# A graph network's node layout: eight consecutive nodes per partition instead of every 128th

## The reference

```python
h = x
for i in range(L):
    hw = jnp.einsum('bnc,cd->bnd', h, weight[i])
    m = jnp.einsum('bjn,bjd->bnd', adj, hw)
    gx = m @ w_ih[i].T + b_ih[i]; gh = h @ w_hh[i].T + b_hh[i]
    xr, xz, xn = split(gx, 3); hr, hz, hn = split(gh, 3)
    r = sigmoid(xr + hr); z = sigmoid(xz + hz)
    n = tanh(xn + r * hn)
    h = (1 - z) * n + z * h
x = layernorm(x + h * mask[:, :, None], axis=-1)   # eps 1e-5
```

## Time and profile before

| | |
|---|---|
| median of 3 runs | 538.66 us (538.38 to 539.0) |
| the profiled execution | 537.98 us |
| its span, first to last instruction | 536.2 us |
| busy: PE / DVE / ACT / POOL | 514.1 / 386.1 / 384.6 / 221.2 us |
| DMA | 85.13 MB, mean 159 GB/s |

### The profile page before, as it was taken

One profiled execution on the slowest core, in us unless ns is written; L12 is line 12 of the kernel. 1 busy time (PEld: TensorE's weight loads), 2 busy tenths in 40 slices (PEclk: granted clock), 3 DMA queues, 4 the chain that ended last, 5 costly groups with the idle time before them and its releaser, 6 DMA issues.

```text
span 536.2 us, 7420 instructions
## 1 busy us (share of the span) xinstructions
PE 514.1 (96%) x2288; PEld 421.5 (79%) x2288; DVE 386.1 (72%) x678; ACT 384.6 (72%) x638; POOL 221.2 (41%) x162
## 2 busy tenths in 40 slices
PE   6999999999999999999999999999999999999970
PEld 4688888888888888888888888888888888888760
DVE  3787666666788886666689886567688887667585
ACT  4668777749776788856886877984986777985444
POOL 2045232344345454432336554232355454344443
PEclk9999999999999999999999999999999999999996
DMA  8941553255732356273662256356472165524212
GB/s 307 382 190 53 213 194 138 91 165 156 238 136 80 122 185 224 82 226 111 198 246 82 65 205 215 117 169 183 137 274 80 60 216 174 185 74 146 90 60 82
DMA packets 78896, 85.13 MB, mean 159 GB/s; under 512 B 3768, under 2 KB 61712, under 8 KB 78864
## 3 DMA queue, kind: packets, MB, share of 16 engines
q1 hardware_dynamic: 78864, 84.73, 47.5%
HBM read 64.27 MB, written 20.45 MB: 158 GB/s over the span
## 4 chain that ended last, share of the span: by engine, by line
PE 92%; DMA 1%; POOL 1%; DVE 1%; issue 1%; SPq 1%; ACT 1%; POOLq 0%; DVEq 0%; ACTq 0%
PE p_S L508 40%; PE p_r L518 6%; PE p_r L522 5%; PE p_r L519 5%; PE p_z L518 5%; PE p_z L522 5%; PE p_z L519 5%; PE p_hn L518 3%; PE p_hn L522 3%; PE p_hn L519 3%; PE p_xn L522 3%; PE p_xn L519 3%; PE p_xn L518 3%; DMA adj_in<-in_adj_dram 1%; PE p_S L478 1%
## 5 line engine op out<-in xcount | busy, mean ns | idle before, releaser
L1272 POOL TENSOR_TENSOR work<-hT,work 128x512 f32<-128x512 f32 x63 | 87.9, 1395 | 266.8 <-ACT work L710 266.8
L508 PE MATMUL p_S<-adj_hi,nat_hi 128*128 128x512 f32 x480 | 187.4, 390 | 0.0
L508 PE MATMUL p_S<-adj_hi,nat_lo 128*128 128x512 f32 x480 | 186.8, 389 | 0.0
L508 PEld LDWEIGHTS p_S<-adj_hi,nat_hi 128*128 128x128 f32 x480 | 90.1, 188 | 18.9 <-DVE nat_lo L894 0.3
L508 PEld LDWEIGHTS p_S<-adj_hi,nat_lo 128*128 128x128 f32 x480 | 90.1, 188 | 18.5
L1141 DVE SCALAR_TENSOR_TENSOR work<-p_hn,bias,work 128x512 f32<-128x512 f32 x62 | 46.5, 750 | 76.2 <-ACT work L710 76.0
L1276 POOL TENSOR_TENSOR work<-work 128x512 f32<-128x512 f32 x63 | 90.1, 1430 | 4.9
L710 ACT ACTIVATE work<-p_r,bsum 128x512 f32<-128x512 f32 x63 | 43.3, 687 | 56.9 <-PE p_r L522 56.2
L931 DVE STREAM_TRANSPOSE work<-hT 128x512 f32<-128x512 f32 x62 | 69.1, 1115 | 2.1
L710 ACT ACTIVATE work<-work,bias 128x512 f32<-128x512 f32 x63 | 45.7, 726 | 31.6 <-DVE work L1145 29.0
L682 ACT ACTIVATE low_words<-adj_in 128x1024 bf16<-128x1024 uint16 x64 | 67.0, 1047 | 1.0
(11 more groups left out here) (148 smaller groups left out, 923.8 us busy)
## 6 DMA issues: line engine op xcount, KB each, us to landing
adj_in<-in_adj_dram SPq DMA_DIRECT2D x72, 512.0 KB, 6.7
bounce<-work SPq DMA_DIRECT2D x62, 256.0 KB, 2.0
low<-bounce SPq DMA_DIRECT2D x62, 256.0 KB, 2.8
x_in<-in_x_dram SPq DMA_DIRECT2D x8, 512.0 KB, 6.8
y<-in_x_dram SPq DMA_DIRECT2D x8, 512.0 KB, 4.4
out_dram<-y SPq DMA_DIRECT2D x7, 512.0 KB, 4.1
out_dram<-y SPq DMA_DIRECT2D x2, 256.0 KB, 2.8
y<-in_L_gnn_w_ih_dram SPq DMA_DIRECT2D x2, 192.0 KB, 7.5
```

The lines of the kernel that those rows point to most:

```text
L508: last = nc.tensor.matmul(p_S[h][:, :], part[:, s, j], adj_hi[:, s, j, half(h)], start=(j == 0 and part is nat_hi), stop=(j == NB - 1 and ...
L1272: nc.gpsimd.tensor_tensor(t_sb[:, h], hT[:, s, half(h)], n_sb[:, h], ALU.subtract).then_inc(d_sub, 1)
```

## The change

A partition p now holds nodes 8p to 8p+7, and block j is nodes 8p+j. So a partition's part of x, of y and of the output is one run of 4 KB in DRAM (2 KB for the two last stores, which move half the blocks each). Tile j of the adjacency is rows 8p+j: still 4 KB a row, now 32 KB apart. The turned layout's column 128k+m is node 8m+k, so both conversions read `adj_in` with a step of eight elements (32 bytes) and write `adj_hi` without gaps, in that order of columns. The mask is loaded straight into its place (32 B at a time), on SP behind x of graph 1; its transpose on PE and its copy on DVE are gone, and DVE waits for it in `residual`. The unused program part (`graph`) is changed to match.

```diff
--- before.py
+++ after.py
@@ -122,12 +122,13 @@
         w_nat = [t[:, 0:(1 + 2 * G) * C].rearrange("p (q d) -> p q d", d=C) for t in places_start]
 
         w_tr = work[:, 2:4].rearrange("p a b c -> p (a b c)")[:, 0:L * (1 + G) * C].rearrange("p (l d) -> p l d", l=L)
-        bias_rows, mask_rows = (t[:, N - P:N] for t in places_start[0:2])
+        bias_rows = places_start[0][:, N - P:N]
 
 
         ident_zero = sem("ident_zero")
         ident_made = sem("ident_made")
         rows_in = sem("rows_in")
+        mask_in = sem("mask_in")
         w_in = [sem(f"w_in{l}") for l in range(L)]
         start_tr = sem("start_tr")
         start_copied = sem("start_copied")
@@ -219,9 +220,11 @@
         CHAIN = 5
         g_S = x_in[:, 1].rearrange("p a b -> p (a b)")
 
-        adj_v = adj.rearrange("b (j p) n -> b j p n", p=P)
-        x_v = x.rearrange("b (j p) c -> b p j c", p=P)
-        out_v = out.rearrange("b (j p) c -> b p j c", p=P)
+        adj_v = adj.rearrange("b (p j) n -> b j p n", p=P)
+
+        mask_v = nodemask.rearrange("b (p j) -> p b j", p=P)
+        x_v = x.rearrange("b (p j) c -> b p j c", p=P)
+        out_v = out.rearrange("b (p j) c -> b p j c", p=P)
 
         def pairs(eng, body):
 
@@ -266,6 +269,13 @@
 
             return t.rearrange("c (p q) -> c q p", q=G)
 
+        def ordered(t):
+
+            return t.rearrange("p (n k) -> p k n", k=NB)
+
+        def blocks_of(t):
+            return t.rearrange("p (k n) -> p k n", k=NB)
+
         def by_block(t):
             return t.rearrange("c (q p) -> c q p", q=G)
 
@@ -285,7 +295,6 @@
             def load_rows():
                 sp.dma_start(bias_rows[0:L * G], b_ih.rearrange("l (q p) -> (l q) p", p=P)).then_inc(rows_in, 16)
                 sp.dma_start(bias_rows[L * G:2 * L * G], b_hh.rearrange("l (q p) -> (l q) p", p=P)).then_inc(rows_in, 16)
-                sp.dma_start(mask_rows[0:B * NB], nodemask.rearrange("b (j p) -> (b j) p", p=P)).then_inc(rows_in, 16)
 
             def load_adj(j):
                 sp.dma_start(adj_in[:, j], adj_v[0, j]).then_inc(adj_loaded[j], 16)
@@ -305,6 +314,7 @@
             load_adj(6)
             load_adj(7)
             sp.dma_start(x_in[:, 1], x_v[1]).then_inc(x_loaded[1], 16)
+            sp.dma_start(mask[:, :].rearrange("p (b j) -> p b j", b=B), mask_v).then_inc(mask_in, 16)
             for j in range(NB):
 
                 wait_adj(sp, 0, j, True)
@@ -428,12 +438,10 @@
 
             def transpose_rows():
 
-                pe.wait_ge(rows_in, 48)
+                pe.wait_ge(rows_in, 32)
                 pe.wait_ge(start_lo, 2)
                 nc.tensor.transpose(p_rows[:, 0:2 * L * G], bias_rows[0:2 * L * G],
-                                    ident[0:2 * L * G, 0:2 * L * G])
-                nc.tensor.transpose(p_rows[:, 2 * L * G:2 * L * G + B * NB], mask_rows[0:B * NB],
-                                    ident[0:B * NB, 0:B * NB]).then_inc(rows_tr, 1)
+                                    ident[0:2 * L * G, 0:2 * L * G]).then_inc(rows_tr, 1)
 
             def join_weights(l):
 
@@ -619,7 +627,8 @@
                         pe.wait_ge(g_nat, (L - 1) * b + l)
                     for h in range(2):
                         for j in range(NB):
-                            last = nc.tensor.matmul(p_S[h][:, :], x_in[:, 0, j], adj_in[:, j, half(h)],
+                            last = nc.tensor.matmul(p_S[h][:, :].rearrange("p (k n) -> p k n", n=P), x_in[:, 0, j],
+                                                    ordered(adj_in[:, j])[:, h * HB:(h + 1) * HB],
                                                     start=(j == 0), stop=(j == NB - 1))
                         last.then_inc(g_s, 1)
                     for h in range(2):
@@ -671,7 +680,7 @@
             def take_adj(p, s, j, first=False):
 
                 act.wait_ge(adj_loaded[j], 16 * (2 * p + s + 1))
-                copy(adj_hi[:, s, j], adj_in[:, j]).then_inc(adj_ready, 2 if first else 1)
+                copy(blocks_of(adj_hi[:, s, j]), ordered(adj_in[:, j])).then_inc(adj_ready, 2 if first else 1)
 
             def check_adj(p, s, j, first, wrapped):
 
@@ -918,12 +927,12 @@
             def take_odd(s, j):
 
                 dve.wait_ge(adj_loaded[j], 16 * (s + 1))
-                nc.vector.tensor_copy(adj_hi[:, s, j], adj_in[:, j]).then_inc(odd_ready, 1)
+                nc.vector.tensor_copy(blocks_of(adj_hi[:, s, j]), ordered(adj_in[:, j])).then_inc(odd_ready, 1)
 
             def take_rows():
                 dve.wait_ge(rows_tr, 1)
-                nc.vector.tensor_copy(bias[:, :, :].rearrange("p a b -> p (a b)"), p_rows[:, 0:2 * L * G])
-                nc.vector.tensor_copy(mask[:, :], p_rows[:, 2 * L * G:2 * L * G + B * NB]).then_inc(rows_out, 1)
+                nc.vector.tensor_copy(bias[:, :, :].rearrange("p a b -> p (a b)"),
+                                      p_rows[:, 0:2 * L * G]).then_inc(rows_out, 1)
 
             def turn(p, g, h):
 
@@ -938,6 +947,7 @@
             def residual(p, s, h):
 
                 if h == 0:
+                    dve.wait_ge(mask_in, 16)
                     dve.wait_ge(y_loaded[s], 16 * (p + 1))
                 dve.wait_ge(bounce_back[h], 16 * (STEPS * p + STEPS - 2 + s + 1))
                 for i in range(HB):
```

## The result

| | before | after |
|---|---|---|
| median | 538.52 us (538.12 to 539.0, 4 runs) | 587.96 us (586.69 to 589.49, 4 runs) |
| ratio to before | | 1.0914, 95% interval 1.0901 to 1.0928 |
| span of the profiled execution | 536.2 us | 587.7 us |

The change costs 49.4 us, or 9%. The forecast was 572 with a range of 552 to 588: right in direction and place, short in size.

The account below looks back on a forecast made before the run. PE was taken to bound the kernel. Changes of pair +32.1, start +2.4, first x -0.4, last stores -0.4 and mask -0.2 make +33.5 us on 537.98, 571.5; the median stands 0.7 higher, so 572, range 552 to 588.

Parts of the forecast that it names:

- What bounds: Whole kernel: PE, 96% busy and 92% of the chain, sets the time; shorter transfers can win only at the two ends.
- The price of a conversion: ACT's adjacency conversions: 1.65 ns an element with the eight-element step, so 1.90 us each instead of 1048 ns.
- D: Extra time of one ACT conversion under the change: taken as 0.85 us, with 0, 0.55 and 1.1 as other cases.
- Where it lies: Steps 6 into 7 and 7 into 0, three changes of pair: seven conversions queued in each, 10.7 us a change, 32.1 in all.
- the formula: Loss over the three changes of pair: 3 x (14 D - 1.2), 32.1 us with the D taken.
- Through which wait: At changes of pair, PE stops for DVE's `t_mul` or ACT ahead of `gates`, three places of 10 to 11 us each.
- The start: First graph's conversions and step 0's sigmoid: 2.4 us lost on ACT; DVE's conversions nothing, up to 2 us without cover.
- The ends: First x load and last two stores: longer runs gain 0.4 us each, within 0 to 1.6 and 0 to 0.8.
- The step costs nothing: Rival at ACT's conversions: D is 0, only the ends move, 537.7 us; chance 0.17.
- the middle penalty: Rival at ACT's conversions: 1.36 ns an element as in the 12-byte row, 559 us; chance 0.25.
- As slow as DVE's transpose: Rival at ACT's conversions: D is 1.1 us, step 0's pause overrun by 0.4 each time, 585 us; chance 0.13.
- It hides in ACT's pauses: Rival: ACT's 151 us without work takes the 48 us penalty, giving 540 to 550 us; chance 0.05.

Follow-up runs that it names:

- Experiment 3: No graph network: ACT, then DVE, copies 1024 elements alone with steps of 1 to 8; ACT 2013 ns at step 4, 2038 ns in the change's form.
- experiment 6: Kernel after the change, but only the first pair's conversions on ACT and DVE read with the step, later ones in a row: 544.09 us, ratio 1.0102.
- Experiment 5: Kernel after the change, but only graph 0's conversions of the second to fourth pair read with the step, others in a row: 561.07 us, ratio 1.0405.
- experiment 9: Kernel after the change plus extra overwritten PE products, 17 ahead of the S_hi wait in step 7, 14 in the next step 0: 590.22 us, ratio 1.0963.
- experiment 7: Kernel after the change, but only ACT's first-pair conversions read with the step, DVE's and all later ones in a row: 542.50 us, ratio 1.0067.
- Experiment 1: Kernel after the change, but both conversions (ACT's and DVE's) read the adjacency tile in a row again: 538.23 us, ratio 0.9982 to before.
- experiment 2: Kernel before, with only the two conversions changed to read every eighth column as in the change: 588.98 us, ratio 1.0926.
- experiment 11: Kernel before, with only the adjacency tiles' 4 KB rows moved to 8 KB apart in DRAM: 543.29 us, ratio 1.0103.

## Why the prediction was right, and where it was short

- **What bounds.** PE's queue sets the time and a change can only matter where PE waits: right. Between the changes of pair, PE's lag stays fixed to 0.1 us.
- **The price of a conversion: the mis-sized term.** Taken was D = 0.85 us (1.90 us a conversion), measured 1.12 (2165 ns). ACT's own row with a 12-byte step was right for that step (1.36 ns an element, 1.32 measured), but the price doesn't grow evenly with the distance. Experiment 3 shows that it reaches its full size at 16 bytes: 1.77 ns on ACT alone, 1.9 in the kernel. I took 1.65 for a place between two rows. The upper bound, 1.9 ns from DVE's block transpose, has the measured size by luck: a DVE copy with the same 16-byte step takes 1072 ns for 1024 elements, 1.05 ns each with its start cost in, against 2.2 for the transpose, so most of that row isn't the price of its step. The upper end of the range rests on that row, so it is luck as well that the range held. The page SBUF — State Buffer of the Trainium skill, section "Door 1: The DMA port swizzle", has steps up to four fp32 elements for free; here four is already at the full penalty and three at half of it, so the measurement decides against the page's limit. Its reason, that a line of 16 bytes has to be used at least twice, fits the rows: with a step of two every line is used twice (+65 ns), with three half of the elements are alone in their line (+502 ns, 0.52 of the full 957), with four all are. That the lines are the cause is not shown beyond this fit.
- **Where it lies.** Three stretches, with seven conversions ahead of the split of x in each half: right. With the measured D the formula gives 3 x (14 x 1.12 - 1.2) = 43.4 us, and 1.4 us more since twice 1.12 overruns ACT's pause of 1.77 us in step 0: 44.8 us; the lag shows 45.6, the medians 43.9 (experiment 6). Experiment 5 hit 561 with 561.1. The 0.8 us between the starts of steps 1 and 2 in the lag reading is that overrun (0.5 by the sum). One term is missing from the sum: it gives 14.9 us for each change, and the first took 16.6, where products at the lower clock held ACT up by some 2 us (experiment 9).
- **Through which wait.** I named DVE's `t_mul` and the wait for r; in the trace PE stops first and longest for `S_hi` (4.1 us) and `hT_hi` (3.5 us), which stand in the same ACT queue, ahead of the split. `t_mul` is left with 0.5 us. The prediction didn't cost these two. What it named stands behind them: `t_mul` is PE's last stop in step 0, and in step 7, once experiment 9 had filled the stop at `S_hi`, PE stopped 1.62 us for the sigmoid of r. So what ends last in a stretch is the work behind the whole queue, and the count of seven conversions held.
- **The start.** Taken was 2.4 us, less 0.4 and 0.2; measured 6.2 in the lag (5.2 and 5.3 in the traces of experiments 9 and 6, which have the same start), 6.5 in experiment 6 by the ratio. With D = 1.12 it was 3.1. Two things were missed. ACT's conversions delay each other through PE: it waits for the tile, the weights' transposes behind it on PE are late, so ACT's own split of the weights is, and the next conversion behind that (tile 6 is converted at 21.74 us, 1.5 us late, and takes 1.0 us longer). And DVE's conversions were put at nothing with "up to 2 us" as the price without cover; experiments 6 and 7 give 1.6 to 1.9 us.
- **The ends.** First x 0.4 us earlier: it was 0.48 (4.18 us against 4.66). Last store to the end of the span: 3.36 us against 3.66, 0.3 for 0.4. Experiment 1 measured 1.0 us for all of it, as summed, with 0.4 to 1.6 open.
- **Rivals.** "The step costs nothing" and "the middle penalty" fall with experiment 3. "As slow as DVE's transpose", 585 us at 0.13, is what happened in size, for a reason that its row didn't hold. "It hides in ACT's pauses" falls with the page: the pauses are still there (ACT is busy for 75%), at other places.

## What to carry to other kernels

Before a layout is chosen for the sake of its transfers, price it on the engine that must read it: here the runs of 4 KB and the mask's new load were worth 1 us together, since only two transfers were waited for, and the reordering read cost 50 (experiment 2). An engine's average share says little; count what stands in its queue ahead of the instruction that others wait for, and subtract the idleness of that stretch alone. If an operation is not in the trace, a row of another engine or another step is a guess and not a bound: ACT's own row was exact at 12 bytes and silent on 32, and the other engine's agreed by chance. A small kernel that runs the copy alone (experiment 3) gave the price to within 6%.

## What the runs showed of the hardware

- ACT, 1024 float32 elements from SBUF to SBUF: 1056, 1121, 1558, 2013, 2017 and 2040 ns for steps of 1, 2, 3, 4, 5 and 8 elements; within 1% the same when the step is on the written side.
- DVE, the same copy: 694, 694, 846, 1072, 1067 and 1082 ns. In a row DVE is a third faster than ACT; with a step of four or more it takes half of ACT's time.
- Loads of 128 rows of 4 KB: with rows 8 KB apart in DRAM the first tile's conversion began at 7.1 us instead of 6.0, and the kernel took 4.7 us more (experiment 11); rows 32 KB apart cost nothing that shows (experiment 1). Why is open.
- Around PE's stops of 2.6 to 4.2 us the granted clock fell to half (1.2 GHz) for 3.4 or 6.8 us and products came every 430 ns instead of every 227. Where another engine's queue sets the end, most of that cost nothing; some 2 us of it came through in the one place where that engine waited for the slow products (experiment 9).
